# Kept rows stored early, normalised rows added to the output by GpSimd's transfers

## What is computed

```
x = x + attention(layernorm(x))
t = layernorm(x)                                   # xn2 in the kernel
t2 = sum over two experts of weight * (relu(t @ W1.T + b1) @ W2.T + b2)
x = x + layernorm(t + t2) * gamma + beta
```

## Time and profile before

| | |
|---|---|
| median of 3 runs | 641.54 us (640.49 to 642.63) |
| the profiled execution's own time | 643.3 us |
| its span, first to last event | 641.5 us |
| PE busy | 92% of the span |
| VectorE, ACT, GpSimd busy | 76%, 68%, 36% |
| mean granted clock of PE | 0.966 |

### The profile page before, as it was taken

The page is one execution under the profiler, slowest core; times in us unless marked ns, Lnnn a source line. Parts: engine busy times, 40 slices in busy tenths (PEclk is TensorE's granted clock), DMA queues, the critical chain, the costliest instruction groups (busy, mean ns, idle before and its releaser), DMA issues.

```text
span 641.5 us, 12423 instructions
## 1 busy us (share of the span) xinstructions
PE 591.1 (92%) x3656; PEld 321.8 (50%) x3656; DVE 485.6 (76%) x1287; ACT 436.5 (68%) x886; POOL 232.7 (36%) x397
## 2 busy tenths in 40 slices
PE   2889999999999999999999999999989999999972
PEld 1634333443443343334334344343389999999730
DVE  3577898999899899899899989988246444555358
ACT  2634787788788888888878888778755544444323
POOL 7110010031422412512332142142177775655545
PEclk9965999999999999999999999999989999999987
DMA  6751812213312411331231230113012432222172
GB/s 196 258 161 50 179 45 80 77 34 94 108 28 77 121 40 48 95 91 31 89 97 39 88 110 27 33 54 103 33 44 73 136 91 68 76 75 79 33 278 114
DMA packets 46621, 56.97 MB, mean 89 GB/s; under 512 B 8366, under 2 KB 25818, under 8 KB 46564
## 3 DMA queue, kind: packets, MB, share of 16 engines
q1 hardware_dynamic: 40580, 45.06, 24.5%
q0 software_dynamic: 4544, 8.53, 3.9%
q10 hardware_dynamic: 1440, 2.69, 1.1%
HBM read 29.28 MB, written 27.16 MB: 88 GB/s over the span
## 4 chain that ended last, share of the span: by engine, by line
PE 64%; DVE 21%; ACT 8%; issue 4%; DMA 2%; POOL 1%; DVEq 0%; ACTq 0%; POOLq 0%
PE pv_psum L1063 13%; DVE mneg L770 11%; PE st_psum L993 10%; PE s_psum L977 10%; PE y_psum L1550 6%; ACT pt L651 4%; PE y_psum L1230 3%; PE side_psum L999 3%; PE side_psum L1025 2%; PE side_psum L1019 2%; ACT xn L669 2%; PE h_psum L1541 2%; PE h_psum L1543 2%; PE h_psum L1542 2%; DVE split L777 2%
## 5 line engine op out<-in xcount | busy, mean ns | idle before, releaser
L770 DVE TENSOR_REDUCE mneg<-s_psum 128x1 f32<-128x512 f32 x512 | 322.9, 684 | 31.9 <-PE s_psum L977 30.4
L651 ACT ACTIVATE pt<-st_psum 128x512 f32<-128x512 f32 x512 | 279.1, 598 | 68.6 <-PE st_psum L993 63.4
L977 PE MATMUL s_psum<-ks,qs 64*128 64x512 f32 x512 | 203.9, 472 | 3.2 <-DVE mneg L770 2.0
L993 PE MATMUL st_psum<-qs,ks 64*128 64x512 f32 x512 | 194.3, 458 | 7.7 <-ACT pt L651 7.6
L977 PEld LDWEIGHTS s_psum<-ks,qs 64*128 64x128 f32 x512 | 83.1, 190 | 109.6 <-DVE mneg L770 87.8
L1063 PE MATMUL pv_psum<-pt,vst 128*16 128x512 f32 x1024 | 135.1, 601 | 0.0
L993 PEld LDWEIGHTS st_psum<-qs,ks 64*128 64x128 f32 x512 | 79.9, 187 | 51.8 <-ACT pt L651 41.3
L1418 ACT ACTIVATE hid<-h_psum,b1c 128x384 f32<-128x384 f32 x68 | 36.9, 581 | 45.9 <-PE h_psum L1543 45.9
L1385 POOL DMA_INDIRECT results<-res,goal_now x51 | 49.9, 979 | 34.5 <-DVE res L1465 22.9
L510 POOL DMA_INDIRECT sent<-xrow,placeu x56 | 54.5, 974 | 16.3 <-issue 16.3
L1550 PE MATMUL y_psum<-w2t,hid 128*128 128x128 f32 x408 | 48.7, 276 | 1.1 <-DVE ysum L1459 1.1
(11 more groups left out here) (219 smaller groups left out, 807.5 us busy)
## 6 DMA issues: line engine op xcount, KB each, us to landing
parts<-split SPq DMA_DIRECT2D x48, 256.0 KB, 3.0
ks<-parts SPq DMA_DIRECT2D x128, 48.0 KB
qs<-parts SPq DMA_DIRECT2D x128, 48.0 KB
lot<-sent SPq DMA_DIRECT2D x18, 198.0 KB
sent<-tail SPq DMA_DIRECT2D x16, 198.0 KB, 5.3
xres<-in_L_attn_x_dram SPq DMA_DIRECT2D x8, 256.0 KB, 3.5
pt<-in_L_ffn_W_dram SPq DMA_DIRECT2D x1, 2048.0 KB, 14.4
got<-results SPq DMA_DIRECT2D x8, 256.0 KB, 6.6
```

The costliest lines, as they stand in the source:

```text
L651: nc.scalar.activation(pt[:, n % PT_SLOTS, (g + 2) % 4, :], st_psum[:, k % ST_BANKS, :], ACT.Exp, scale=SCALE).then_inc(exp_done, 1)
L770: nc.vector.tensor_reduce(mneg[:, (n // 4) % 2, at:at + 1], s_psum[:, k % S_BANKS, :], AX_X, ALU.max, negate=True).then_inc(max_done, 1)
L977: mm(s_psum[:, k % S_BANKS, :], qs[rows, c, P * (n % 4):P * (n % 4) + P], ks[rows, c, g, :], start=True, stop=True).then_inc(s_made, 1)
L993: mm(st_psum[:, k % ST_BANKS, :], ks[rows, c, g, P * (n % 4):P * (n % 4) + P], qs[rows, c, :], start=True, stop=True).then_inc(st_made, 1)
```

## The change

The kept rows go to the output by themselves: ACT issues the stores of batches 0 to 5 after beat 134, behind the two loads, once `rows_sent` shows these batches' rows landed, and the store of batch 6 ahead of the expert loops. At the end VectorE no longer adds the kept rows of batches 0 to 6. GpSimd issues, for each of these batches, a transfer of `normed` to the output that adds to what stands there (`accum_op=ALU.add`), three batches behind its `scale`, and three in a row after the last. Minus the mean is made by VectorE (`negate_mean`) instead of GpSimd. The last batch keeps its way, with SP's store.

```diff
@@ attention, scalar
             if T == GROUPS * B + ST_LAG:
                 early.load_vectors(act)
+                early.store_residuals(act, 0, EARLY_BATCHES)
@@ class Early
+    def store_residuals(self, act, first, after):
+        act.wait_ge(self.kept.rows_sent, 16 * 2 * TILES * after)
+        for b in range(first, after):
+            act.dma_start(self.out_tiles[:, b], self.kept.xres[:, tiles(b), :]).then_inc(self.residual_out, 16)
+
@@ experts, sync
-        for b in range(B):
-            sp.wait_ge(fin_done, b + 1)
-            sp.dma_start(out_tiles[:, b], got[:, 0, tiles(b), :]).then_inc(stored, 16)
-        sp.wait_ge(stored, 16 * B)
+        sp.wait_ge(fin_done, 1)
+        sp.dma_start(out_tiles[:, B - 1], got[:, 0, tiles(B - 1), :]).then_inc(stored, 16)
+        sp.wait_ge(stored, 16)
+        sp.wait_ge(residual_out, 16 * (B - 1))
+        sp.wait_ge(added_out, 16 * (B - 1))
@@ experts, gpsimd
         def scale(b):
             pool.wait_ge(m3_done, b + 1)
             nc.gpsimd.tensor_tensor(vareps3[:, b], moments3[:, b, :, 1], kept.eps[:], ALU.add).then_inc(v3_done, 1)
-            nc.gpsimd.tensor_tensor(minus_mean[:, b], kept.zero4[:], moments3[:, b, :, 0], ALU.subtract)\
-                .then_inc(v3_done, 1)
-            pool.wait_ge(v3_done, b * 2 + 2)
+            pool.wait_ge(v3_done, b + 1)
             nc.gpsimd.tensor_tensor(rstd3[:, b], vareps3[:, b], kept.power[:], ALU.pow).then_inc(r3_done, 1)
             if b < B - 1:
                 pool.wait_ge(r3_done, b + 1)
+                pool.wait_ge(mean_done, b + 1)
                 nc.gpsimd.tensor_tensor(shift3[:, b], minus_mean[:, b], rstd3[:, b], ALU.mult)\
                     .then_inc(shift_done, 1)
+        def add_out(b):
+            pool.wait_ge(g_done, b + 1)
+            pool.wait_ge(residual_out, 16 * (B - 1))
+            pool.dma_start(out_tiles[:, b], normed[:, b], accum_op=ALU.add).then_inc(added_out, 16)
+
         for b in range(B):
             scale(b)
+            if b >= COMPLETE_LAG:
+                add_out(b - COMPLETE_LAG)
+        for b in range(B - COMPLETE_LAG, B - 1):
+            add_out(b)
@@ experts, scalar
         turns, first = counts_of("scalar", act)
+        early.store_residuals(act, EARLY_BATCHES, B - 1)
@@ experts, vector
         def complete(b):
             dve.wait_ge(n_done, b + 1)
-            at = tiles(b)
             nc.vector.tensor_tensor(normed[:, b], normed[:, b],
                                     gammab[:].unsqueeze(1).to_broadcast([P, TILES, D]), ALU.mult).then_inc(g_done, 1)
-            dve.wait_ge(g_done, b + 1)
-            nc.vector.tensor_tensor(got[:, 0, at, :], normed[:, b], kept.xres[:, at, :], ALU.add).then_inc(fin_done, 1)
 
         def complete_last(b):
-            dve.wait_ge(v3_done, b * 2 + 2)
+            dve.wait_ge(mean_done, b + 1)
...
+        def negate_mean(b):
+            dve.wait_ge(m3_done, b + 1)
+            nc.vector.tensor_scalar(minus_mean[:, b], moments3[:, b, :, 0], -1.0, None, ALU.mult).then_inc(mean_done, 1)
+
         for b in range(B):
             combine(b)
             if b >= COMPLETE_LAG:
                 complete(b - COMPLETE_LAG)
+            negate_mean(b)
         for b in range(B - COMPLETE_LAG, B - 1):
             complete(b)
         complete_last(B - 1)
```

More of the change, by code:

```diff
@@ L1132, in __init__ @@
                  x_psum, y_at, rows_stored, b2_loaded, lot, goals, marks, lot_loaded, lot_turned, goals_taken, xh_done,
-                 xl_done, sem):
+                 xl_done, out_tiles, residual_out, sem):
+        self.out_tiles, self.residual_out = out_tiles, residual_out
         self.lot, self.goals, self.marks = lot, goals, marks
@@ L1318, in experts @@
         sem(n) for n in ("n_done", "g_done", "fin_done", "stored", "shift3_done"))
+    mean_done, residual_out, added_out = (sem(n) for n in ("mean3_done", "residual_out", "added_out"))
+    out_tiles = out.rearrange("b (p j) d -> p b j d", p=P)
     def y_at(h):
@@ L1325, in experts @@
                   y_at, rows_stored, b2_loaded, lot, goals, marks, lot_loaded, lot_turned, goals_taken, xh_done,
-                  xl_done, sem)
+                  xl_done, out_tiles, residual_out, sem)
     def counts_of(name, eng):
@@ L1368, in sync @@
             sp.dma_start(got[:, 0, tiles(b), :], got_from[:, 0, b]).then_inc(got_in[b], 16)
-        out_tiles = out.rearrange("b (p j) d -> p b j d", p=P)
-        for b in range(B):
-            sp.wait_ge(fin_done, b + 1)
-            sp.dma_start(out_tiles[:, b], got[:, 0, tiles(b), :]).then_inc(stored, 16)
-        sp.wait_ge(stored, 16 * B)
+        sp.wait_ge(fin_done, 1)
[3 more added lines that the diff above has]
+        sp.wait_ge(added_out, 16 * (B - 1))
     def gpsimd(pool):
```

## The result

The kernel after takes 650.73 us (median of 4 runs, 649.14 to 652.58), the one before beside it 641.01 (4 runs): ratio 1.0138, 95% interval 1.0109 to 1.0168. By the medians it is 9.7 slower, where +1.0 was forecast, and it lies above the range. The profiled execution took 650.35, its span is 648.6.

A forecast was written before the change was run, and what follows sets the result against it. GpSimd was to replace VectorE as the bound of the last stage. Its +0.1 there and +0.9 from ACT's six stores made +1.0 on the median 641.54: 642.5 us, range 639.0 to 646.4.

The forecast's parts named there:

- GpSimd takes VectorE's place: Last stage: GpSimd becomes the bound, giving back about all of the 4.3 us that VectorE could save.
- the sum: GpSimd's last stage from 622.4: batches 7.0, the last without shift 1.4, seven issues 7.7; last issue ends at 638.5.
- the cheap one: GpSimd's issue of an addition: costs 0.6, like L1151's, so the kernel is faster, 639.2; chance 0.22.
- the costly one: GpSimd's issue of an addition: costs more than 1.25; at 1.41 it adds 2.2, giving 644.7; chance 0.28.
- The chain that ended last: End of the kernel: this chain was to end in GpSimd's transfers, as a sign that the forecast is right.
- The store of batch 6: ACT ahead of the expert loops: 0.5 hides in ACT's idle 2.59; without that cover it would cost 0.5.
- Step one: ACT at beat 134: six stores at 0.45 each delay the copy L643 and PE, +0.9, ends 0.2 and 1.2.
- Step two: Last addition: lands 2.45 after its issue ends, 1.67 as a plain store plus 0.78 for reading 256 KB.
- The third rival: Last three additions: issued 1.1 apart, each holding the transfer engines 2.0, the third 1.8 late, 644.3; chance 0.08.
- Step three: End of the span: it follows the last landing by 0.7, as SP's last store showed in the kernel before.
- my sum: End of the span: last issue 638.5, landing 2.45 and 0.7 more give 641.65, +0.1 against 641.5.

The follow-up runs named there:

- e1: Changed kernel with the six early stores of kept rows issued by SP instead of ACT: 648.42 us, ratio 1.0093 to the kernel before.
- e3: Changed kernel with GpSimd's seven adding transfers made plain, so seven batches' kept rows are missing from the result: 647.56 us, ratio 1.0095 to the kernel before.
- e2: Kernel before plus only ACT's early stores of seven batches' kept rows, its last stage adding and storing as before: 646.80 us, ratio 1.0087.
- e7: Changed kernel with GpSimd also waiting for its seven additions to land before its program ends: 655.71 us, ratio 1.0219 to the kernel before.
- e5: Changed kernel with only two batches added by transfers, the others by VectorE, and early stores by SP: 641.04 us, ratio 0.9983 to the kernel before.
- e6: Changed kernel with only four batches added by transfers, the others by VectorE, and early stores by SP: 642.82 us, ratio 1.0015 to the kernel before.
- e9: Kernel before with only the negation of the mean moved from GpSimd to VectorE: 642.65 us, ratio 1.0014.
- e8: Kernel before plus one plain 2 MB load issued by GpSimd after VectorE's last operation, SP waiting for it too: 651.14 us, ratio 1.0156.
- e4: Kernel before plus one small GpSimd memset after VectorE's last operation: 645.87 us, ratio 1.0063.

## Why the prediction was wrong

| | forecast | measured |
|---|---|---|
| middle: ACT's six stores, each | 0.45 | 0.72 |
| middle: PE later by | +0.9 | +3.6 |
| an addition's issue on GpSimd | 1.1 | 0.9 to 1.0 |
| batch 3's moments to the end of the last issue | 16.1 | 16.3 |
| from there to the last landing | 2.45 | 5.1 |
| from there to the end of the span | 0.7 | 3.5 |

**Right.** GpSimd takes VectorE's place as the limit of the last stage, in rounds of 2.85, and VectorE waits for ACT and so for GpSimd. That chain came out 0.2 from the sum: 640.01 - 623.68 = 16.3 against 638.5 - 622.4. That it came so near is luck in part: the seven issues took 6.4 in all, not 7.7, and what lies between them 9.9, not 8.4. Of the two rivals about the issue neither came true: at 0.9 to 1.0 it is dearer than the cheap one's 0.6 and under the 1.25 from which the costly one decides. The chain that ended last runs through GpSimd's issues, as forecast. The store of batch 6 shows no cost: with the six early stores given to SP, and the seventh still on ACT (e1), the middle is 139.1, no longer than before.

**Step one that failed: "each store is issued by ACT ... I take 0.45 ... +0.9".** The ends were 0.33 and 0.51. Behind a load of 512 KB the first three issues took 0.44 to 0.52, as priced, but the fourth 1.22 and the two after it 0.89 and 0.67. What the step left out altogether is the clock: a PE that stands for 3.4 is granted the lower clock right after, and that is the last 1 of the +3.6. My remark that "the 1.5 MB share the transfer engines" with others, "for which nobody waits", looked at who waits for the data and not at who waits for the issue.

**Step two: the landing, 2.45 with ends of 1.2 and 4.** The addition was priced as a plain store and the reading of 256 KB at full rate. It holds the engines 1.92 where the plain transfer holds them 0.69. The third rival, slow additions that pile up, had nearly this number, though by luck (2.0 each, taken from the time to land of a plain store), and a chance of 0.08, since the engines were used 0.40; the place decides, though: the last three come in a row and have no gap between them to fill. The landing was 2.6 later than forecast. Of this 0.6 is that even an addition by itself lands 4.0 - 0.94 = 3.06 behind the end of its issue. The other 2.0 are the pile: by the rival's working with the measured numbers, 2 x (1.92 - 0.89) = 2.06. The additions ahead have no part in it: the first of the last three still landed 3.8 after its issue began, no later than one by itself. What SP's store adds to the pile no run separates.

The Trainium skill, page Collectives: The Full Stack, section The bandwidth ceiling, has two read descriptors per chunk for a reduction and one for a copy. The dearer issue (0.94 against 0.60) and the longer hold agree with it in direction; the packets listed per addition (144, as many as of SP's plain store, and 80 of GpSimd's plain transfer) don't show the second reading.

**Step three: "the span ends ... 0.7 behind a landing".** This is the step that I could have got right from the trace at hand. The line L150 of before has GpSimd's DRAIN ending 0.25 behind SP's and 6 behind the last root. Had I read it, every issue that GpSimd makes after the last root would have had to be counted against 6 and not against 2.45 + 0.7: the last issue at 638.5 and 6 is 644.5, 3 above my sum, before anything is known of additions. The Trainium skill, page VectorE: DVE Perf Modes, section The DRAIN you can't avoid, puts the DRAINs that stand around every kernel at some 12 ns on all five engines; if it means these, SP's (13 ns) agrees, VectorE's and ACT's are entered early here and end within 0.1 us of the engine's last operation, and GpSimd's doesn't agree: it ends 6.0 us behind its last.

So the two places divide the 9.4 thus: 3.6 for the stores in ACT's stream, and 5.8 for the last stage, of which 0.2 are in the chain of issues, 2.6 in the landing and 2.8 in the DRAIN behind it; 0.1 was forecast, the rest is rounding. Slower landing and DRAIN are not independent. Without the first, in e3, the span still ended 6.8 behind the last issue, where my sum has 3.15 from there to the end.

What stays open is why the fourth issue on ACT's queue waits. Full transfer engines alone don't explain it. In e1 they were as full (share 1.02 from 450 on), and SP's issues took 0.65 at most. In before, ACT issues eight loads of 256 KB in a row at 609, with the share at 1.02 from 611 on, and none took longer than 0.64:

```profile
L1428 ACTq DMA_DIRECT2D got<-results x8: 361/460/638, 609.1 to 612.7; - x8
```

So a queue of several 256 KB transfers ahead doesn't explain it either. The one sign in the traces points at the two loads of vectors ahead on ACT's queue: in after the fourth issue ends at 463.08 and the load of b2 lands at 462.9, the fifth ends at 464.00 and the load of gamma lands at 463.8, and in e2, e3 and e7 these times pair up as well, within 0.3. That ACT waits for these landings is not shown; no run puts the stores ahead of the loads.

## What to carry to other kernels

Read the closing instructions of each engine before moving work to the end of its stream: on GpSimd the end costs about 6 us from its last instruction here, so its last task has to be done well before the others are, and a transfer of its own that lands late holds the end still longer. A transfer isn't only its data: the engine that issues it stands for the time of the issue, and six issues behind a large load took 4.3 us between two steps of a chain that everything waits for; on a queue whose engine has nothing else to do they were free (e1). An addition made by a transfer costs the transfer engines nearly three times a plain store. Seven of them, three in a row at the end, made the kernel slower; two or four, early, left its time about where it was (e5, e6).

## What the runs showed of the hardware that was not expected

- GpSimd's closing DRAIN ends 6.0 to 6.5 behind its last instruction (before and e2 to e7, in e7 behind its last wait; e9), and 3.0 to 3.3 behind the landing of its own last transfer where that is later (e1, e8, after). VectorE's and ACT's end within 0.1 of their last operations; SP's takes 0.013.
- An adding transfer of 256 KB: issue 0.94, 1.92 of all 16 engines, 4.0 to land by itself; the same transfer without the addition 0.60, 0.69 and 2.4.
- Six stores of 256 KB issued by ACT behind a load of 512 KB: 0.44 to 1.22 each; eight loads of the same size on ACT's queue 0.36 to 0.64 each.
- The clock near the start is not the same in every execution. Windows of before and of after, in a stretch in which the two programs do the same:

```profile
58.00:62.00 4.00, 4.00 (x16) 2.64 (x16) 2.22 (x4) 2.06 (x4) 0.00 (x0) 0.50 0.00 0
```

```profile
58.00:62.00 4.00, 3.88 (x29) 1.76 (x27) 3.80 (x7) 3.60 (x8) 0.00 (x0) 1.00 0.00 0
```

The lower level lasts to 65 or so in before, e1, e4, e5 and e6, and only to 55 to 58 in after, e2, e3, e7, e8 and e9, which have nothing in common in their changes. It moves everything behind it by some 3 us in a single profile, and is why the accounts above go by stretches between operations that both kernels have.
